# One block for the whole program: the last batch's scores, exponentials and products in one written order with the second part

## What is computed

```python
x = x + xattn(layernorm(x), ctx, ctx)     # 16 heads of 16, softmax over 1601 context rows, projections q, k, v, o with biases
x = x + attn(layernorm(x))                # 64 x 64: scores = -softplus(b) * (pos - sigmoid(a) * 64) ** 2 per head, softmax, @ value, @ W_out
x = x + ffn(layernorm(x))                 # (shared SwiGLU of 512 + mean of two of eight gelu experts by token position) / 2
```

## Time and profile before

| | us |
|---|---|
| median of three runs | 1529.22 |
| profiled execution, whole | 1530.81 |
| its span, first to last instruction | 1528.6 |
| PE busy in the span | 1470.1 |
| last value projection of batch 31 over | 1239 |
| turn 31 on PE | 1241.3 to 1261.4 |
| barrier between the parts | 1266.1 |
| first unit of the second part | 1290.7 |
| first X (values of chunk 0) | 1310.6 |
| last variance of the second layer norm (v3) | 1453.7 |
| last matmul over | 1525.3 |

### The profile page before, as it was taken

The page is one execution under the profiler, slowest core; times in us unless marked ns, Lnnn a source line. Parts: engine busy times, 40 slices in busy tenths (PEclk is TensorE's granted clock), DMA queues, the critical chain, the costliest instruction groups (busy, mean ns, idle before and its releaser), DMA issues. The chain is left out here.

```text
span 1528.6 us, 56227 instructions
## 1 busy us (share of the span) xinstructions
PE 1470.1 (96%) x23420; PEld 1241.6 (81%) x23420; DVE 999.5 (65%) x3958; ACT 921.0 (60%) x1825; POOL 447.8 (29%) x564
## 2 busy tenths in 40 slices
PE   7999999999999999999999999999999987899899
PEld 4788888888888888888888888888888873566588
DVE  5766767676666776767666666676677745654345
ACT  4455666566566665666666666666666663587483
POOL 4433333333333333333333333333333302300043
PEclk9999999999999999999999999999999999799999
DMA  5644444444444444444444444444444314100012
GB/s 160 198 115 111 115 113 116 110 118 112 115 116 109 118 114 112 113 117 117 111 117 114 116 111 113 117 113 112 112 114 116 74 25 143 40 1 1 1 56 83
DMA packets 91759, 156.24 MB, mean 102 GB/s; under 512 B 44897, under 2 KB 55905, under 8 KB 91489
## 3 DMA queue, kind: packets, MB, share of 16 engines
q1 hardware_dynamic: 91216, 151.57, 36.8%
q0 software_dynamic: 288, 1.05, 0.2%
HBM read 69.61 MB, written 4.19 MB: 48 GB/s over the span
## 5 line engine op out<-in xcount | busy, mean ns | idle before, releaser
L674 DVE CUSTOM_DVE_ANT_0 junk<-bank,mask_q 128x400 bf16<-128x400 f32 (+1 forms) x1024 | 547.3, 571 | 183.9 <-issue 176.1
L620 ACT ACTIVATE probs<-bank 128x512 f32<-128x512 f32 (+1 forms) x832 | 467.8, 596 | 120.4 <-PE bank L808 111.1
L590 POOL CAST ctx_hi<-ctx_raw 128x400 fp32r<-128x400 f32 x248 | 122.7, 524 | 785.4 <-PE bank L765 785.4
L808 PE MATMUL bank<-qstack,kstack 104*128 104x128 f16 (+1 forms) x3328 | 289.3, 220 | 4.2 <-ACT probs L620 3.4
L765 PE MATMUL bank<-wv_hi,ctx_hi 128*128 128x256 f32 (+1 forms) x832 | 279.8, 336 | 0.0
L785 PE MATMUL bank<-kstack,qstack 96*128 96x400 f16 (+1 forms) x1024 | 267.2, 336 | 4.3 <-DMA qstack<-q_parts 2.2
L640 ACT ACTIVATE v<-bank 128x256 f32<-128x256 f32 (+1 forms) x416 | 159.8, 384 | 180.8 <-PE bank L765 174.6
L663 DVE SCALAR_TENSOR_TENSOR k_lo<-bank,bk,k_hi 128x400 f16<-128x400 f32 (+1 forms) x256 | 162.0, 633 | 160.6 <-ACT k_hi L630 160.5
L808 PEld LDWEIGHTS bank<-qstack,kstack 104*128 104x128 f16 (+1 forms) x3328 | 213.8, 99 | 64.6 <-issue 16.6
L630 ACT ACTIVATE k_hi<-bank,bk 128x400 f16<-128x400 f32 (+1 forms) x256 | 152.4, 595 | 175.0 <-PE bank L755 166.5
L593 POOL TENSOR_TENSOR ctx_lo<-ctx_raw,ctx_hi 128x400 fp32r<-128x400 f32 x248 | 253.8, 1045 | 0.0
(11 more groups left out here) (171 smaller groups left out, 1629.8 us busy)
## 6 DMA issues: line engine op xcount, KB each, us to landing
ctx_raw<-in_ctxT SPq DMA_DIRECT2D x32, 1602.0 KB, 6.9
kstack<-k_hi SPq DMA_DIRECT2D x512, 100.1 KB, 2.2
kstack<-k_lo SPq DMA_DIRECT2D x256, 100.1 KB, 2.2
weight<-in_w SPq DMA_DIRECT2D x18, 256.0 KB, 2.7
x<-in_xT SPq DMA_DIRECT2D x8, 512.0 KB, 8.5
qstack<-q_parts SPq DMA_DIRECT2D x192, 16.0 KB, 5.3
out_yT<-y SPq DMA_DIRECT2D x8, 256.0 KB, 3.2
weight<-in_sw SPq DMA_DIRECT2D x3, 512.0 KB, 5.9
```

The lines of the kernel that those rows point to most:

```text
L590: nc.gpsimd.tensor_copy(c_hi[:, k, s0:s0 + n], raw[:, k, s0:s0 + n]).then_inc(ctx_hi, 1)
L620: nc.scalar.activation(probs[kt % NP][0:m, GROUPS * h:GROUPS * (h + 1), :], st[h][0:m, :], ACT.Exp, scale=DK ** -0.5 / (UP * UP)).then_inc ...
L674: nc.vector.tensor_tensor_reduce(junk[i % SM][:, 0:n], sm[i % SM][:, 0:n], w["mask_q"][:, s0:s0 + n], 1.0, -3.0e38, ALU.add, ALU.max, part ...
L808: mm = nc.tensor.matmul(st[h][0:m, g * PW:(g + 1) * PW], kstack[b.slot][0:KROWS, p, kt * P:kt * P + m], qstack[b.slot][0:KROWS, p, :], sta ...
```

## The change

The second part's block goes. There is one block for the program, and on each engine the second part's order follows the first part's turns 0 to 30 directly. Turn 31 is taken out of the turns and written into the second part's strings: l is the last product of batch 30, s0 to s25 the scores and p0 to p12 the products of batch 31, e0 to e25 the exponentials, j and u `join` and `outputs` of batches 30 and 31. On PE the first 51 steps (`PE_HEAD`) stand in each branch of the `pe.If`, the rest (`PE_BODY`) behind it. W0 is the 17th step, M0, W1, V0, W2, S0 and T0 follow among the scores; M1, the first A, p11 and p12 open the body, and W3 comes behind the third A.

SP waits for the counters that say that turn 30 is over, and then loads x at once; POOL waits for x before it loads the selectors, and for all 32 outputs before it splits weights; DVE sets its constants (a0) after x has come. The first W waits for the last value copy, the first unit for all exponentials of batch 31, the second for its join. Distances use banks 2 and 3, statistics 4 and 5 (before the reverse), and the routed experts go with the distances' banks. Allocations are reordered, so that tiles that turn 31 still reads lie under tiles which are written later; these moves alone are left out of the diff. The preload of ACT's table at the start of the second block goes. The orders after the first chunk are new as well: units stand in pairs, and F and G come later on the whole (with v3 done, G1, two F2, G2, four F3, G3, K and P are left, where before it was G2, four F3, G3, K and P).

```diff
-        tail(nc, ins, bank, attn_out, out_done, wo, bo_all, mean_w, eps_col, ident, out_dram, sem)
+        rest = tail(nc, ins, bank, attn_out, out_done, wo, bo_all, mean_w, eps_col, ident, out_dram, d, sem)
+
+        def program(eng, name):
+            early = before[name](eng)
+            cross[name](eng, early, rest[name])
...
-            for n in range(B):
+            for n in range(B - 1):
...
-        for n in range(B - 4, B):
+        for n in range(B - 4, B - 1):
...
+        rest(act, {"e": lambda i, _: exponentials(at(B - 1), i // 2, i % 2)})
...
-        join(at(B - 1))
-        outputs(at(B - 1))
-
-    def tensor(pe, early):
+        rest(dve, {"j": lambda i, _: join(at(B - 2 + i)), "u": lambda i, _: outputs(at(B - 2 + i))})
...
-            products(at(B - 1), KT - 1)
-
-
+            rest_head({**last_products, "s": lambda i, _: scores(at(B - 1), i // 2, i % 2, masked)})
+
+
+        rest_head, rest_body = rest(pe)
+        last_products = {"l": lambda i, _: products(at(B - 2), KT - 1), "p": lambda kt, _: products(at(B - 1), kt)}
...
         with pe.If(rows_all == S):
             run(masked=False)
         with pe.Else():
             run(masked=True)
+        rest_body(last_products)
...
+    PE_HEAD = """l0 s0 s1 s2 s3 p0 s4 s5 p1 s6 s7 p2 s8 p3 s9 s10 W0 s11 s12 p4 s13 p5 M0 W1 s14 s15 V0 s16 s17 W2 S0 s18 s19 p6 p7
+        p8 s20 s21 p9 s22 s23 T0 s24 p10 s25"""
+    PE_BODY = """M1 A0 p11 p12 V1 A0 A0 W3 A0 S1 A0 A0 T1 A0 A0 M2 X0 X0 U0 X0 X0 V2 A1 O0 S2 A1 A1 Z0 T2 A1 A1 M3 A1 m0 A1 A1 V3 v0
+        X1 X1 U1 X1 X1 S3 O1 A2 F0 A2 T3 A2 Z1 A2 A2 m1 A2 A2 F0 A2 v1 F0 X2 X2 U2 F0 X2 X2 A3 O2 A3 Z2 A3 A3 m2 A3 A3 F1 A3
+        A3 v2 G0 U3 F1 X3 X3 F1 X3 X3 F1 O3 F2 Z3 m3 F2 v3 G1 F2 K0 F2 K1 F3 K2 F3 P0 G2 K3 F3 K4 F3 K5 P1 G3 K6 P2 P3 P4 K7
+        P5 P6 P7"""
+    DVE_ORDER = """j0 u0 a0 W0 C0 W1 N0 W2 R0 C1 D0 j1 u1 N1 D0 W3 D0 D0 R1 D0 D0 D0 D0 b0 C2 N2 D1 O0 R2 D1 D1 Z0 D1 D1 C3 D1 c0 D1 D1
+        n0 N3 h0 O1 R3 D2 F0 D2 D2 Z1 D2 D2 G0 c1 D2 D2 F0 D2 n1 F0 G0 G0 O2 F0 D3 h1 G0 D3 Z2 D3 D3 c2 D3 D3 F1 D3 D3 n2 r0
+        h2 G1 F1 G1 F1 G1 F1 O3 G1 F2 Z3 c3 F2 n3 r1 G2 h3 G2 F2 G2 F2 P0 F3 P0 P1 G2 F3 P1 P2 P2 r2 G3 G3 F3 G3 F3 G3 P3 P3
+        r3 K0 K1 Y0 Y1 K2 K3 K4 K5 Y2 P4 P4 K6 Y3 K7 P5 P5 Y4 P6 P6 Y5 P7 P7 Y6 Y7"""
+    ACT_ORDER = """e0 e1 e2 e3 e4 e5 e6 e7 e8 e9 e10 e11 e12 e13 Q0 e14 e15 I0 e16 e17 S0 e18 e19 e20 e21 e22 e23 T0 e24 e25 B0 Q1 I1
+        B0 B0 E0 E0 B0 E0 S1 B0 B0 E0 E0 T1 B0 B0 E0 E0 E0 X0 X0 Q2 L0 X0 X0 I2 B1 U0 E1 S2 B1 B1 E1 T2 B1 B1 E1 E1 E1 B1 Q3
+        B1 B1 q0 E1 E1 I3 E1 i0 X1 X1 H0 X1 X1 L1 U1 S3 B2 F0 B2 B2 E2 E2 T3 E2 B2 B2 G0 E2 E2 B2 B2 q1 E2 E2 F0 B2 i1 E2 F0
+        X2 G0 G0 X2 L2 X2 X2 U2 F0 B3 H1 G0 B3 E3 E3 B3 B3 E3 E3 B3 B3 q2 E3 E3 F1 B3 B3 i2 E3 E3 H2 G1 L3 U3 F1 X3 G1 X3 F1
+        X3 G1 X3 F1 G1 F2 q3 F2 i3 H3 G2 G2 F2 G2 K0 F2 P0 K0 K1 F3 P0 P1 G2 K1 F3 P1 K2 K2 P2 P2 G3 G3 K3 K3 F3 G3 K4 K4 F3
+        G3 P3 P3 K5 K5 P4 P4 K6 K6 P5 P5 P6 P6 K7 K7 P7 P7"""
...
-        proj, ln_bank, ab, vb = bank[0:2], bank[2:4], bank[4:6], bank[6:8]
+        wval, wout = (sb(n, [P, NK, D]) for n in ("wval", "wout"))
+        wspan = sb("wspan", [P, NK, 2 * H])
+        sel_a, sel_b = sb("sel_a", [P, PAIRS, P], F32R), sb("sel_b", [P, PAIRS, P], F32R)
+        head_ones = sb("head_ones", [P, 32])
+        sb1, sb3 = sb("sb1", [P, FT]), sb("sb3", [P, FT])
+        sb2, b1, b2 = sb("sb2", [P, NK]), sb("b1", [P, E, NK]), sb("b2", [P, E, NK])
+        class_bias = sb("class_bias", [P, E, NK])
+        bias_a, bias_b = sb("bias_a", [P, NK]), sb("bias_b", [P, NK])
+        weight = [sb(f"weight{i}", [P, NK * HS]) for i in range(2)]
+        sw1, sw3, sw2 = parts("sw1", [P, NK, HS]), parts("sw3", [P, NK, HS]), parts("sw2", [P, FT, D])
+        tokens = parts("tokens", [P, NK, E, NC])
+        gate = [sb(f"gate{i}", [P, CW]) for i in range(2)]
+        gate_parts = parts("gate", [P, FT, CW])
+        w1 = [parts(f"w1_{i}", [P, NK, D]) for i in range(W_SLOTS)]
+
+        proj, ab, ln_bank, vb = bank[0:2], bank[2:4], bank[4:6], bank[6:8]
+        routed_bank = [ab, vb]
...
+            sp.wait_ge(d["shift_done"], 2 * B)
+            sp.wait_ge(d["v_proj"], KT * B)
+            sp.wait_ge(d["ctx_lo"], SPLIT * B)
+            sp.wait_ge(d["st_ready"], NST * (B - 1))
+            sp.wait_ge(d["pv_done"], KT * (B - 1))
+            for p in range(PAIRS):
+                sp.wait_ge(d["kstack_in"][1][p], 16 * 3 * (B // 2))
...
         def gpsimd(pool):
+            pool.wait_ge(x_in[0], 16)
             for name, tile in (("c_sel_a", sel_a), ("c_sel_b", sel_b)):
                 pool.dma_start(tile[:], ins[name].rearrange("r (p m) -> r p m", m=P)).then_inc(s["sel_in"], 16)
+            pool.wait_ge(out_done, B)
             pool.wait_ge(s["rows_done"], 1)
...
+            def constants_in(_, i):
+
+                dve.wait_ge(x_in[0], 16)
+                nc.vector.tensor_copy(ident_r[:], ident[:]).then_inc(s["turn_ready"], 1)
+                nc.vector.memset(packed[:].bitcast(F32), 0.0).then_inc(s["packed_zero"], 1)
+                dve.wait_ge(s["packed_zero"], 1)
+                nc.vector.memset(packed[:, :, ONE_ROW:ONE_ROW + 1].bitcast(F32), 1.0).then_inc(s["turn_ready"], 1)
+                nc.vector.memset(vbd[:], 0.0).then_inc(s["vbd_zero"], 1)
...
+                if c == 0:
+                    pe.wait_ge(d["wo_in"], 3 * 16)
+                    pe.wait_ge(d["v_done"], KT * B)
...
+                    if c == 0:
+                        pe.wait_ge(d["exp_done"], NST * B)
                 if i == 1:
+                    if c == 0:
+                        pe.wait_ge(d["both_done"], 2 * B)
...
+            head_count = {}
+
+            def head(last_turn):
+                emitted.update(dict.fromkeys("WZFG", 0))
+                head_count.clear()
+                run_order(PE_HEAD, {**table, **last_turn}, head_count)
+
+            def body(last_turn):
+                run_order(PE_BODY, {**table, **last_turn}, head_count)
+
+            return head, body
```

133 lines of the change are left out of this document (44 added, 89 removed).

## The result

The changed kernel takes 1517.63 us (median of four runs, 1516.59 to 1519.5); the kernel before, run beside it, 1529.88. The ratio is 0.9918 [0.9904, 0.9932], so it is faster by 12 us. Its profiled execution took 1517.93 us, 1.9 over its span.

What follows compares the result with a forecast made beforehand. PE, busy 96% of 1528.6 us, was taken as the bound, with its idle time at the seam to be gained. Terms: 12.8 - 2 = 10.8 us off, span 1517.8, plus 0.6 gives 1518.4; range 1508 to 1527.

Steps and rivals of the forecast that it cites:

- First term: From the last turn to the first distance unit: unit done at 1280.0 in place of 1293.2, 13.2 us ahead.
- W0 at 1247.2: Last turn on PE: the first projection starts behind s10, which waits for the ninth exponential, and runs 1247.2 to 1250.7.
- The jump, 4.4 us: Between s25 and M1: the jump past the masked branch holds PE 4.4 us, bounds 0 and 4.8.
- Half clock behind it, 2.2 us: After the jump: M1 and the first unit take 3.6 and 0.9 us in place of 1.8 and 0.5.
- Second term, the unit stage: First unit to X0: 19.6 us in place of 17.4, costing 2.2 (bounds 0 and 4.4); PE owes 1.8 less.
- I take the old pack's 4.9 us: Unit stage: chunk 1's pack on DVE, with POOL splitting weights beside it, lasts 4.9 us as in the old trace.
- Third term, X0 to v3: The three following chunks: 130.2 us if no wait grows, 2 us lost, so 132.2; bounds 5 gained and 11 lost.
- Fourth, without price: Drain and barrier, table load, bank swap, extra ACT table changes and POOL's selector loads: no cost or gain.
- A: Jump between s25 and M1 costs little: 6.6 us come back, 1511.8, down to 1506; chance 0.18.
- B: Attention stages: missing filling not repaid, some 8 of the 10.8 us given back, 1526; chance 0.17.
- C: Attention chunks: sparser PE put to half clock in each, X0 to v3 147 us, total 1533.4; chance 0.05.
- D: Last turn and second part's first chain only stretch each other over ACT; units at 1290 again, 1529; chance 0.04.

Runs made afterwards that it cites:

- pool_earlier: Changed kernel with POOL splitting the three shared-expert weights from the first row copy on, without waiting for all outputs: 1512.5 us, ratio 0.9872.
- body_in_branch: Changed kernel with the body of PE's order written into each branch, so the jump comes after the last matmul: 1512.83 us, ratio 0.9892.
- body_pool_earlier: Changed kernel with PE's body in both branches and the shared-expert weights split from the first row copy on: 1510.59 us, ratio 0.9874.
- seam_only: Changed kernel with its one block and new order up to chunk 0's last unit, the old order behind that: 1520.9 us, ratio 0.9935.
- units_first: Changed kernel with T1 and R1 put behind all eight units of chunk 0 in all three orders: 1521.73 us, ratio 0.9931.
- pool_later: Changed kernel with POOL's weight splitting held back until the second row copy in place of the first: 1517.56 us, ratio 0.9907.
- short_jump: Changed kernel with the masked branch cut to a single wait, so PE jumps past only one instruction: 1511.22 us, ratio 0.9874.
- orders_only: Kernel before, its two blocks kept, with only the new written orders less batch 31's steps: 1533.01 against 1531.65 us, ratio 1.001.
- pool_quarters: Changed kernel with POOL's cast and subtraction of each weight made in four quarters of the columns: ratio 0.992.
- body_pool_quarters: Changed kernel with PE's body in both branches, shared-expert weights split earlier, and POOL's casts and subtractions in quarters: 1513.91 us, ratio 0.9891.

## Why the prediction was right, point by point

The total was right, 1518.4 against 1517.6, and so was the mechanism of the seam. But that it came within 1 us is luck: two errors of 6 and 8 us cancel. In the prediction's own steps (times on each trace's own axis; T31 of the kernel after lies 0.7 us earlier than before, which is a gain of the first part's length and not of the change):

**First term.** *W0 at 1247.2*: it started at 1248.98. A product among the scores waited 0.63 us for DVE's join, which I had not priced, and PE's clock was 0.50 from 1244 to 1246. The kernel after and, under it, `pool_earlier` in the same two stretches behind T31 (columns as in rows 2):

```profile
1242.00:1244.00 2.00, 1.28 (x39) 0.83 (x36) 1.89 (x7) 1.25 (x3) 0.00 (x0) 0.89 0.88 259
1244.00:1246.00 2.00, 2.00 (x44) 1.61 (x41) 1.52 (x4) 1.09 (x2) 0.54 (x1) 0.50 0.86 272
```
```profile
1241.81:1243.81 2.00, 1.28 (x42) 0.89 (x40) 1.89 (x7) 1.25 (x3) 0.00 (x0) 1.00 0.88 260
1243.81:1245.81 2.00, 1.91 (x62) 1.43 (x64) 1.18 (x4) 1.61 (x4) 0.13 (x1) 1.00 0.77 250
```

Eleven of the traced kernels have this order of the last turn, and in all eleven PE is busy for 1.28 us of the first stretch, with the same wait of 0.63. Six of them then have a clock of 0.50, five (`pool_earlier`, `body_in_branch`, `body_pool_earlier`, `seam_only`, `units_first`) keep 1.00; so the dip is a property neither of the order nor of what PE did just before. It costs 1.2 us: W0 starts 10.4 to 10.5 us behind T31 with it and 9.3 without (10.7 in `pool_later`, where it comes a little earlier). *The load of x hidden by W0*: it went out at 1240.96 and DVE's constants stood 0.33 us for it at 1245.18, so the cover held. The scores ended at 1273.55, where I had 1271.1. *The jump, 4.4 us*: the gap is 3.18. *Half clock behind it, 2.2 us*: M1 took 2.81 in place of 1.9 and the unit 1.84 in place of 1.03 (`body_in_branch`); 1.7 in sum. The lateness of the one and the shortness of the others cancel: the first unit was done at 1280.4, forecast 1280.0. The two kernels without the gap show the step whole: from W0's start to the end of the first unit both take 26.8 us, the kernel after 31.4. That is 4.6 us, where I had 4.4 + 2.2. (T31 to A0 is 35.1 in `body_in_branch` and 36.3 in `short_jump`, for 40.1; the 1.2 us between the two are the dip ahead of W0, which `short_jump` has too. In three of the six kernels with the gap M1 takes 3.75 us, twice its length, so what the clock adds varies as well.) (The Trainium skill, page Runtime: NRT & Kernel Launch, section Instruction fetch mechanics, says that a taken branch to code that is not loaded stalls for a fetch; the far and the short jump, 3.2 us and none, agree with it. The about 51 ns that its page Advanced Engine Details and Errata, section Control Flow Timing, gives for a branch can stand for the short one only; no row here resolves it.)

**Second term, the unit stage, failed in size.** Forecast were 19.6 us from the first unit's end to X0, measured were 25.7 (1280.4 to 1306.1). The failing step is "I take the old pack's 4.9 us": it took 7.7 (1293.3 to 1301.0), and N1 ahead of it 3.7 in place of 1.3, which I had not priced at all. These two make 5.2 of the 6.1 us. I had seen one row of this, 1.38 against 0.29 in the earlier trace rows, and took the sum over the old pack as if it were the price of POOL working beside it. But what a step pays depends on which instruction of POOL it meets, and when. In the kernel before (DVE, then POOL)

```profile
1299.60 1.29 DVE L1286 TENSOR_TENSOR t_h<-t_xc,t_rstd 128x512 f32<-128x512 f32 x2 [1.18 <-ACT t_rstd L1117]
```
```profile
1298.29 2.79 POOL L1087 TENSOR_SCALAR weight<-weight 128x1024 f32<-128x1024 f32 x1 [0.62 <-DMA weight<-in_sw]
```

N1 falls into the middle of POOL's halving of a weight, which doesn't hold it there, and the last pack steps fall beside the short splits of the routed weights, with 1 us of idle time between them. The change's new wait for all outputs puts POOL's start at 1284.8, 0.6 us ahead of N1, so that N1 and the pack meet the long splits. `orders_only`, which has no such wait, meets a long split too (N1 3.91), so the new order alone can bring it about. In `body_in_branch` the same order meets POOL in another phase: N1 is held (3.45), but most of the pack falls into the halving of 1285.92 to 1288.71, four steps in its middle take their 0.20 to 0.23, and the pack takes 4.2 us; hence A0 to X0 23.7 there. `pool_later` takes the overlap away and gives 20.3, `pool_quarters` keeps it and shortens each piece, and gives 23.3. The rest of the term stood: W3 from 1284.8 (forecast 1285.5), the first exponential at 1288.6 (1289.5).

**Third term, X0 to v3, failed in the other direction.** Forecast 132.2, measured 124.1. Two parts. "2 us lost" was wrong: idle time there fell by 1.0. And PE's busy time fell by 18.0 us, where the moved matmuls account for 13.0 by count. The other 5 are in the first chunk most of all: 230 matmuls took 32.05 us busy at a clock of 0.89, 226 now take 26.26 at 1.00. Not all of that is the clock: `pool_later`, the new order at 0.90, takes 29.04, and `seam_only`, the old one at 0.91, 31.20. I had the clock rows of before and used them for a rival that was slower; that the change could as well take a stretch of half clock away stood nowhere in my sum, only inside the bound of "5 gained". `orders_only` puts this stretch down to the new order, with 125.5 us in the old two blocks.

**Fourth, without price**, held: v3 to the end grew by 10.8 us, where 11.2 were moved there; ACT's extra table loads don't show on the chain.

The sum of errors: +0.4 (first; +1.1 if counted from T31), +6.1 (second), -8.1 (third), -0.4 (end), which is -2.0 on the span of 1517.8, where 1516.0 was measured.

**The rivals.** *A* (the jump costs little) fell as a statement on this kernel, and `short_jump` shows what it would have been: 1511.2, against my 1511.8. That they agree is chance again: its stages are 6.1 us shorter than those of the kernel after, but 3.8 of these are up to A0, 4.0 in the unit stage, where DVE meets POOL in another phase, and 1.5 are lost from X0 to v3. *B* (missing filling not repaid) and *C* (half clock in the chunks) fell: 124.1 us, full clock in all four stages. *D* (the parts only stretch each other) fell for the seam: 11.4 us gained up to A0. It has something to it one stage later, where the unit stage gave back 7.7, though by way of POOL and not ACT.

What stays open: what decides where the clock dips. The order alone doesn't, nor what PE did just before (the eleven kernels above), and each kernel was traced once, so executions of one kernel could not be compared. The new order's X0 to v3 varies by 5 us from kernel to kernel (124.1 to 129.5), in part with these dips, so single traces can't assign differences of this size to an edit.

## What to carry to other kernels

When a change moves the start of POOL's work, list which of DVE's steps will lie beside it afterwards, and bound the wait of each by the length of POOL's instruction, not by the steps that happened to be slow before. The jump past the masked turns cost PE some 3 us wherever nothing else was waited for; such a jump belongs beside a wait, or the tail in both branches. An order that frees 19 us in one stretch may only have moved them: cut the trace at fixed events to its very end before counting a gain.

## What was not expected of the hardware

- A step of DVE with all its operands in SBUF that starts beside a cast or subtraction of POOL waits until that instruction ends, whatever its own size: 2.22 us for two columns (0.16 alone), 2.13 for 64 (0.22), 2.02 for 128 (0.29), each ending within 0.15 us of POOL's. The two 128x512 instructions of N1 (0.68 each alone) end 0.55 after the POOL instruction that they met. It goes the other way too: the subtraction that began during N1's first instruction took 2.67 us in place of 2.34, the cast during its second 1.49 in place of 1.04. Steps that read a PSUM bank don't change (1.39, 0.22), nor do the reciprocals (0.55).
- POOL's halving of a weight, in place from SBUF to SBUF, holds DVE only in part of its 2.79 us. A small step that starts in its first 1.0 us ends 1.05 to 1.13 us after the halving's start (0.96 for two columns in `pool_later`, 1.00 for 64 in `pool_quarters`, 0.45 in the kernel after). Behind that steps run at their own length: N1 in the kernel before starts 1.3 us after it and keeps 1.29, and in `body_pool_quarters` N1's second instruction starts 0.5 us after it and takes 1.52 of the 2.63. From 1.9 us on the steps with one operand are held again, until it is over (L1322, 0.90 in place of 0.20 in the kernel after; L1327, 0.74 in place of 0.23 in `body_in_branch`), and those with two are not (0.16 in `pool_later`).
- The stall of the taken jump goes with the code that it passes: 2.8 to 3.4 us past the masked turns in six kernels, nothing past one instruction.
- The same matmuls with the same busy time before them ran on at a granted clock of 1.00 in five kernels and at 0.50 in six, in the next 2 us, and W0 started 1.2 us later for it (1.4 in `pool_later`).
